# First cross attention: latent keys behind the context keys, latent values as one product over 96 stacked rows

## The reference, cut to what matters

```python
def _L0_xattn_ref(latents, context, Wq, Wk, Wv, Wo, q_norm_w, k_norm_w):
    HEADS, KV_HEADS, HEAD_DIM, EPS = 32, 8, 128, 1e-6
    kv = jnp.concatenate([context, latents], axis=1)      # 512 + 32 keys
    q = (latents @ Wq).reshape(...); k = (kv @ Wk).reshape(...); v = (kv @ Wv).reshape(...)
    q = rms_norm(q, q_norm_w); k = rms_norm(k, k_norm_w)
    scores = einsum('bhgqd,bhkd->bhgqk', qg, k) / sqrt(HEAD_DIM)
    probs = softmax(scores)                               # over all 544 keys
    out = einsum('bhgqk,bhkd->bhgqd', probs, v)
    return out @ Wo
```

## Time and profile before

| | us |
|---|---|
| Median of 3 runs (lowest, highest) | 1724.15 (1723.53, 1724.68) |
| Span of the profiled execution | 1722.3 |
| PE busy | 1599.7 (93%) |
| DVE busy | 900.3 (52%) |
| ACT busy | 610.9 (35%) |
| POOL busy | 349.7 (20%) |

### The profile page before, as it was taken

The page is one execution under the profiler, slowest core; times in us unless marked ns, Lnnn a source line. Parts: engine busy times, 40 slices in busy tenths (PEclk is TensorE's granted clock), DMA queues, the critical chain, the costliest instruction groups (busy, mean ns, idle before and its releaser), DMA issues. The chain is left out here.

```text
span 1722.3 us, 23860 instructions
## 1 busy us (share of the span) xinstructions
PE 1599.7 (93%) x8374; PEld 1325.3 (77%) x8374; DVE 900.3 (52%) x1704; ACT 610.9 (35%) x1036; POOL 349.7 (20%) x476
## 2 busy tenths in 40 slices
PE   6899999999999999978988899999999999876798
PEld 5678888888888887777546688888888888655686
DVE  5724454454544444565337355555555555556565
ACT  5523233332333333443126333333333333331343
POOL 3622111221112211041005421121121121101000
PEclk9999999999999999989579999999999999988899
DMA  7200000000000011252134000000000001230342
GB/s 258 74 28 27 9 20 20 8 27 8 20 20 8 27 51 50 98 202 91 58 114 154 7 26 13 12 24 12 12 24 14 11 25 50 97 118 0 133 162 86
DMA packets 25349, 94.57 MB, mean 55 GB/s; under 512 B 4422, under 2 KB 4550, under 8 KB 20680
## 3 DMA queue, kind: packets, MB, share of 16 engines
q1 hardware_dynamic: 25292, 93.82, 15.1%
HBM read 92.24 MB, written 1.57 MB: 54 GB/s over the span
## 5 line engine op out<-in xcount | busy, mean ns | idle before, releaser
L51 PE MATMUL c1a_kbanks<-c_wkv_lo_r,c_cT_hi 128*128 128x512 f32 x256 | 106.4, 416 | 3.5 <-PEq L368 3.5
L51 PE MATMUL c0a_kbanks<-c_wkv_lo_r,c_cT_hi 128*128 128x512 f32 x256 | 105.5, 412 | 1.5 <-PEq L368 1.5
L51 PE MATMUL c0a_vbank<-c_wkv_lo_r,c_cT_hi 128*128 128x512 f32 x256 | 105.1, 410 | 0.0
L968 DVE TENSOR_REDUCE c0a_ss<-c0a_sq 128x4 f32<-128x512 f32 x64 | 43.9, 685 | 116.4 <-ACT c0a_sq L888 102.3
L879 ACT ACTIVATE c0a_p<-c0a_sbank,c0a_nmax 128x544 f32<-128x544 f32 x62 | 44.5, 718 | 162.9 <-DVE c0a_nmax L922 162.9
L734 POOL TENSOR_TENSOR c0a_ms<-c0a_ss,c0a_const 128x4 f32<-128x4 f32 x64 | 12.7, 199 | 440.9 <-DVE c0a_ss L968 440.9
L968 DVE TENSOR_REDUCE c1a_ss<-c1a_sq 128x4 f32<-128x512 f32 x64 | 43.8, 685 | 111.5 <-ACT c1a_sq L888 111.5
L53 PE MATMUL c1a_kbanks<-c_wkv_hi,c_cT_lo_r 128*128 128x512 f32 x256 | 100.9, 394 | 0.0
L53 PE MATMUL c0a_kbanks<-c_wkv_hi,c_cT_lo_r 128*128 128x512 f32 x256 | 100.5, 393 | 0.0
L52 PE MATMUL c1a_kbanks<-c_wkv_hi,c_cT_hi 128*128 128x512 f32 x256 | 100.5, 392 | 0.0
L53 PE MATMUL c0a_vbank<-c_wkv_hi,c_cT_lo_r 128*128 128x512 f32 x256 | 100.1, 391 | 0.0
(11 more groups left out here) (461 smaller groups left out, 4442.2 us busy)
## 6 DMA issues: line engine op xcount, KB each, us to landing
g_stage<-in_l_wq SPq DMA_DIRECT2D x16, 1024.0 KB, 4.8
c_cT_lo<-in_ctx SPq DMA_DIRECT2D x64, 256.0 KB, 2.5
c_wkv_lo<-in_l_wo SPq DMA_DIRECT2D x16, 1024.0 KB, 4.8
e_stage<-in_e_w SPq DMA_DIRECT2D x20, 768.0 KB, 4.2
c_wkv_lo<-in_l_wkv SPq DMA_DIRECT2D x16, 512.0 KB, 5.5
m_stage<-in_mix_ffn SPq DMA_DIRECT2D x10, 768.0 KB, 4.3
m_traw<-in_mix_out SPq DMA_DIRECT2D x1, 1792.0 KB, 11.3
f_graw<-in_lora_g SPq DMA_DIRECT2D x1, 1536.0 KB, 7.3
```

What stands on the lines that cost most here:

```text
L51: nc.tensor.matmul(out, a[0], b[1], start=start, stop=False)
L968: nc.vector.tensor_reduce(ss[:, k % 2, :], sq[:, :].rearrange("p (h d) -> p h d", h=UNIT_H), AX.X, ALU.add).then_inc(k_summed, 1)
```

## The change: what it does

1. Latent keys. `kT` hi and lo get 544 columns for each head; POOL rounds the 32 latent keys of each head into the last 32 columns and subtracts for the rest (`latent_keys`, once for each unit, behind `q_lo`). `q_whole` and its copy go. `score` issues each of its three split products in two pieces of 272 columns, one in each bank of `sbank`. Maximum and exponential read two sides of 272.
2. Latent values. A rounded part and a rest are stored (two transfers of 1 MB; the rest is computed by DVE at the end of `queries`, `vl_rest`). `vlat` has 96 rows: hi, lo, hi, loaded by three transfers for each unit. The transposed latent probabilities stand beside it in `pTs`: hi, hi, rest. ACT writes the two rounded copies (`tail_heads`, between its copy of the values and that of the keys), DVE subtracts for the rest in place of its copy of 32 rows. `pv` ends with one fp32r matmul over 96 rows.
3. POOL and DVE wait for both stores at the start of `attend`, and in `finish` ACT's order is two exponentials, two `tail_heads`, then the output weights.

```diff
@@ queries
+                    sp.wait_ge(vl_rest, 2 * TT)
+                    for part in range(2):
+                        sp.dma_start(g["vlat_dram"][part].rearrange("(t p) n -> p t n", p=P),
+                                     as_f32(vl[:, part, :, :])).then_inc(vl_stored, 16)
...
+                if vl is not None:
+                    for j in range(2 * TT):
+                        half, t = divmod(j, TT)
+                        dve.wait_ge(vl_ready, j + 1)
+                        nc.vector.tensor_tensor(vl[:, 1, t, half * UW:(half + 1) * UW], pbank[j][:],
+                                                as_f32(vl[:, 0, t, half * UW:(half + 1) * UW]),
+                                                ALU.subtract).then_inc(vl_rest, 1)
@@ attend, SP
-                            sp.wait_ge(vl_stored, 16)
-                        sp.dma_start(vlat[:, hf, :],
+                            sp.wait_ge(vl_stored, 32)
+                        for row, part in enumerate((0, 1, 0)):
+                            sp.dma_start(as_f32(vlat[row * ROWS:(row + 1) * ROWS, hf, :]),
@@ attend, POOL
-                    if tail:
-                        nc.gpsimd.tensor_copy(flat(q_whole), mine)
...
+                def latent_keys(b, hf, u):
+                    own = klatT[:, hf * UNIT_H:(hf + 1) * UNIT_H, bass.ds(b * SEQ, SEQ)]
+                    nc.gpsimd.tensor_copy(kT[0][:, hf, :, CTX:KEYS], own).then_inc(kl_hi, 1)
+                    pool.wait_ge(const_set, 2)
+                    pool.wait_ge(kl_hi, u + 1)
+                    nc.gpsimd.tensor_tensor(kT[1][:, hf, :, CTX:KEYS], own, as_f32(kT[0][:, hf, :, CTX:KEYS]),
+                                            ALU.subtract).then_inc(kl_lo, 1)
...
+                if tail:
+                    pool.wait_ge(vl_stored, 32)
@@ attend, PE
-                    last = mm3(nc, bank[:, 0:CTX], tuple(h[:, ahf, k, :] for h in q),
-                               tuple(h[:, ahf, k, :] for h in kT), True, True)
                     if tail:
-                        last = nc.tensor.matmul(bank[:, CTX:KEYS], q_whole[:, ahf, k, :],
-                                                klatT[:, ahf * UNIT_H + k, bass.ds(at, SEQ)],
-                                                start=True, stop=True)
+                        for qp, kp in ((0, 1), (0, 0), (1, 0)):
+                            for side in range(2):
+                                last = nc.tensor.matmul(bank[:, side * CTX:side * CTX + HALF], q[qp][:, ahf, k, :],
+                                                        kT[kp][:, ahf, k, side * HALF:(side + 1) * HALF],
+                                                        start=(kp == 1), stop=(qp == 1))
...
-                        last = nc.tensor.matmul(bank[:, 0:HD], pT[0:SEQ, k % 2, CT, :],
+                        last = nc.tensor.matmul(bank[:, 0:HD], pTs[:, k % 2, :],
                                                 vlat[:, ahf, k * HD:(k + 1) * HD], start=False, stop=True)
@@ attend, ACT
+                def tail_heads(a, k, bank):
+                    act.wait_ge(pt_done, a + 1)
+                    need(act, o_done, a - 1)
+                    for row in range(2):
+                        nc.scalar.activation(pTs[row * ROWS:(row + 1) * ROWS, k % 2, :],
+                                             bank[0:SEQ, TAIL_T:TAIL_T + P], ACT.Copy).then_inc(pt_tail, 1)
@@ attend, DVE
                     if tail:
-                        last = nc.vector.tensor_copy(pT[0:SEQ, k % 2, CT, :], tail_bank[0:SEQ, TAIL_T:TAIL_T + P])
+                        dve.wait_ge(pt_tail, 2 * a + 2)
+                        last = nc.vector.tensor_tensor(pTs[2 * ROWS:STACK, k % 2, :],
+                                                       tail_bank[0:SEQ, TAIL_T:TAIL_T + P],
+                                                       as_f32(pTs[0:ROWS, k % 2, :]), ALU.subtract)
```

More of the change, by code:

```diff
@@ L620, in attend @@
         p = s.sb("p", [P, 2, KEYS])
-        pT = s.sb("pT", [P, 2, CT + 1, P])
+        pT = s.sb("pT", [P, 2, CT, P])
+        pTs = s.sb("pT_stack", [STACK, 2, P], F32R) if tail else None
         on = s.sb("on", [P, 2, HD])
@@ L673, in run, with sides @@
             finish()
+        def sides(bank):
+            return bank[:, :].rearrange("p (a n) -> p a n", a=2)[:, :, 0:HALF]
         def parts(b, hf):
@@ L826, in step @@
                             need(pe, pt_ready, a)
-                            score(a, sbank, ahf, k, (b - 1 if hf == 0 else b) * SEQ)
+                            score(a, sbank, ahf, k)
                         elif k > 0:
@@ L848, in finish @@
                     for k in range(2):
-                        score(LAST + k, scores[k], 1, k, at)
+                        score(LAST + k, scores[k], 1, k)
                     o_transpose(LAST - 1, 1, obank)
@@ L859, in finish @@
                             if k + 2 < UNIT_H:
-                                score(LAST + k + 2, scores[k % 2], 1, k + 2, at)
+                                score(LAST + k + 2, scores[k % 2], 1, k + 2)
                         for k in (pair, pair + 1):
@@ L877, in exponential @@
                     need(act, pt_done, a - 1)
-                    src = sm[:, k % 2, :] if mask is not None else bank[:, 0:KEYS]
-                    nc.scalar.activation(p[:, k % 2, :], src, ACT.Exp, bias=nmax[:, k:k + 1],
-                                         accum_out=rsum[:, k:k + 1]).then_inc(p_ready, 1)
+                    if mask is not None:
+                        src, dst = sm[:, k % 2, :], p[:, k % 2, :]
+                    else:
+                        src, dst = sides(bank), p[:, k % 2, :].rearrange("p (a n) -> p a n", a=2)
+                    nc.scalar.activation(dst, src, ACT.Exp, bias=nmax[:, k:k + 1],
+                                         accum_out=rsum[:, k:k + 1]).then_inc(p_ready, 1)
+                def tail_heads(a, k, bank):
+                    if not tail:
+                        return
+                    act.wait_ge(pt_done, a + 1)
[3 more added lines that the diff above has]
+                                             bank[0:SEQ, TAIL_T:TAIL_T + P], ACT.Copy).then_inc(pt_tail, 1)
                 def step(b, hf):
@@ L901, in finish @@
                 def finish():
-                    for k in range(UNIT_H):
-                        exponential(LAST + k, k, scores[k % 2])
-                        if k % 2:
-                            wo.make_hi(act, k // 2)
+                    for pair in range(0, UNIT_H, 2):
+                        for k in (pair, pair + 1):
+                            exponential(LAST + k, k, scores[k % 2])
+                        for k in (pair, pair + 1):
+                            tail_heads(LAST + k, k, scores[k % 2])
+                        wo.make_hi(act, pair // 2)
                 run(act, step, finish)
```

50 lines of the change are left out of this document (32 added, 18 removed).

## The result

The changed kernel takes 1686.95 us (median of 4 runs, 1686.35 to 1689.8), the kernel before, in runs on the same chip, 1724.41 (4 runs, 1723.53 to 1725.72). The ratio is 0.9781, 95% interval 0.9767 to 0.9795: faster by 2.2%. 1686 was forecast, with a range of 1678 to 1706. The profiled execution has a span of 1684.8 us, 37.5 less than before; forecast was 37.9.

The account below looks back on a forecast made before the run. PE, busy 537.76 of 540.00 us in `c0`'s steps, was taken as the bound. From the 1722.3 us span: -39.2 steps, -1 `finish`, +2.3 border = 1684.4; the median lies 1.85 above, so 1686, range 1678 to 1706.

Parts of the forecast that it names:

- The score: Score in `c0`'s steps: six 272-column fp32r pieces take 0.76 us instead of 1.03 with aftermath, saving 0.27 a step.
- The value tail: End of `pv`: one 96-row fp32r product costs 0.20 us instead of 0.59, saving 0.39 a step.
- the first fp32r behind fp32: Surcharge on the first fp32r matmul after fp32 ones: 0.09 us seen behind the old score, 0.08 put on the tail.
- the old product's 0.59: Old 32-row product in `pv`: 0.59 us, of which 0.17 lost ahead and 0.42 from its start to the score.
- R1: Value tail: 96 rows make PE drain as for 32; 17 us less gained, 1703 us; chance 0.12.
- R2: Ring ACT copies, keys, L912, `ot_place`, `pv` closes; PE waits some 0.3 us a step, 1704 us; chance 0.06.
- R3: Score: each of six pieces waits for its own weight load, 0.316 us a piece, 1755 us; chance 0.03.
- The border: Between the two blocks: two stores delay PE and DVE, a loss of 2.3 us, bounds 0.7 and 5.
- PE's later start: At the border: SP's wait for a DVE subtraction and a second store issue start PE 1.1 us later.
- the wait of 1.2 us ahead of the first `kt`: After the border: `kn` ends at 114.6, PE reaches the first `kt` at 113.4 and waits 1.2 us.
- or the clock falls in the longer idle stretch: At the border: one of the reasons given, with slower stores, for the upper bound of 5 us loss.
- `finish`: Remaining 5 `pv` and 4 scores, where PE waits for others: a gain of 1 us, 0 to 3.

Follow-up runs that it names:

- keys only: Changed kernel with the latent keys and six-piece score alone, old value tail kept: 1715.44 us, ratio 0.9951 to the kernel before.
- 512 + 32: Changed kernel with each split product of the score cut into pieces of 512 and 32 columns instead of two of 272: 1706.6 us, one run.
- 4 x 136: Changed kernel with the score in twelve pieces of 136 columns instead of six of 272: 1722.1 us, one run.
- 32 and 64 rows: Changed kernel with its last value product over only the first 32 or 64 of the 96 stacked rows: 1705.7 and 1714.8 us, one run each.
- eight more copies: Changed kernel with eight extra ACT copies of 32 x 64 behind the two, making ten, for which DVE waits: 1688.9 us, one run.
- the early stores: Changed kernel with the latent values stored in four halves, each issued as soon as its two banks are ready: 1688.46 us, ratio 0.9775.
- both removed: Changed kernel with the four early stores plus eight unused 128x512 products on PE behind the last query matmul: 1686.15 us, ratio 0.9756.
- the two halves: Changed kernel with only the keys part, 1715.44 us (ratio 0.9951), and with only the values part, 1696.28 us (ratio 0.9844).

## Why the prediction was right

**The bound.** PE is busy for 489.97 of 491.60 us at clock 1.00 in the steps, and it waits for nobody in them. So what the two parts save on PE arrives in full: 0.653 us a step against 0.66.

**The score**: 0.76 and no surcharge behind it was the step, 0.81 and none (0.24 against 0.227) is measured. A piece inside the row costs 0.125 as worked out from 256 and 512 columns (0.126). The first pair costs 0.31 instead of 0.25. Saved: 0.13 + 0.08 = 0.21, not 0.27. Of these 0.21 only 0.16 are the score's own (the step with keys only); 0.05 come with the 96 rows, for the 32-row product had slowed the score's first pair too.

**The value tail**: 0.14, not 0.20, and none of the gap: saved 0.45, not 0.39 (0.49 with what it takes off the score). Both misses are nearly one: I put 0.08 for "the first fp32r behind fp32" on the tail, and 0.06 falls on the next matmul. Nor is it the change of type. With 512 + 32 and with 4 x 136 all matmuls at that place are fp32r, and the value matmul behind still pays 0.08 and 0.06. What these places have in common is a short matmul ahead (32, 128 or 136 columns). That the longer one's weights then come late is the reading that fits; no experiment took the load apart from the matmul. The split of the old product's 0.59 was also off: "about 0.2" the product and "nearly 0.4" the change of rows. The runs give 0.29 for the rows (and 0.05 behind, in the score), 0.16 for plain fp32 and 0.14 for the product.

**R1** (96 rows turn the array) is refuted by 0.81 + 0.14. Its price was close: 0.29 a step was worked out, and 32 and 64 rows lengthen the step by 0.31 and 0.34. That is partly luck, since both terms of the difference (0.49 and 0.20) were 0.06 too high (0.43 and 0.14 measured). **R2** (the ring closes) is refuted: in the steps no load of `pv` waits for `ot_place`. The prediction counted the cover to the product; to the load, which is what waits, 0.78 us is left, and it took eight more copies to use that up. **R3** (loads not hidden) is refuted: pieces are 0.125 apart, with load records of 0.19, and pieces of 136 columns 0.112.

**The border**: +2.3 was forecast and +2.9 came, but by another way. PE's later start was right (+1.1; idle time grew by 1.29). The step that failed is the wait of 1.2 us ahead of the first `kt`. DVE is even 1.0 later than forecast (`kn` ends at 115.60, forecast 114.6), yet PE waits only 0.14, since it is itself 1.6 us late through the clock. I had that among the bounds ("or the clock falls in the longer idle stretch") and not in the sum. The clock's 1.6 and the wait for `kn` lie side by side, so removing the wait alone left the clock's part: with the early stores DVE is free, and the tile is still slow. Removing the clock's part alone was not run; with both removed the first `kt` comes 8.27 after PE's start, as before the change.

**`finish`**: 1 was taken, with a bound of 3, and it gave 3.4. Four scores and five tails at the steps' prices are 4 x 0.21 + 5 x 0.45 = 3.1 if all lay on the path. By the estimate from the two halves the change gave 2.4, inside the bound, and 1.0 is the clock that had fallen in the profile of before. Of the whole, then, about 1 us is no merit of the change.

The errors, +0.8 in the steps, +0.6 at the border, +0.4 in the queries, -2.4 in `finish` and +1.0 behind (untouched blocks, where the same kernel differed by 3.4), leave 0.4. 0.9 of the last lies in `c0`'s output block, which was granted a mean clock of 0.96 before and 0.92 after. That the sum is closer than its parts is luck: the gain in `finish` happens to pay for the others. The mechanism in the steps, which bring the whole net gain, was right. (The prediction's own range of 1679 to 1694 is a little narrower than its named bounds add up to, about 1677 to 1696.)

## What to carry to other kernels

Where one engine is busy for all of a loop, look for the instruction whose neighbours start late, and not for the one that lasts long: a product over few rows cost over 0.3 us beside its own time, and stacking the three terms of its split into one product of 96 rows took that away, for two small copies on an engine that had time to spare. Cut an uneven length into equal pieces as long as each stays above the time of the next one's weight load, and price a short piece with the start of the matmul behind it. When you count how much time a chain has before PE waits, count to the weight load and not to the product. At a border that leaves PE idle, read the granted clock of the first work behind it before you name a wait.

## What the runs showed of the hardware

- A product of 32 or of 64 rows between products of 128 rows costs 0.17 us ahead, 0.12 behind it and 0.03 to 0.05 more on the pair behind that; the step is 0.31 and 0.34 longer. One of 96 rows costs none of it.
- fp32r matmuls that each load new weights start 0.125 apart with 272 columns and 0.112 with 136. Behind a piece of 32 columns the next starts after 0.03, but its own 512 columns then take 0.32 and not 0.23.
- The weight load of `pv` waits for `ot_place`, not the product: with ten copies it stood idle 29 times, up to 0.17 late, and the step did not get longer.
- ACT copies of 32 x 64 from PSUM start 0.106 apart, with records of 0.20 to 0.22. The two of 32 x 128 take 0.29 each (0.58 until the next instruction), with records of 0.27. Why only the smaller ones overlap stays open.
- PE's clock behind a pause. At the border nine runs had 2.2 to 2.8 us without work, and in all nine the first tile ran partly at the 1.2 GHz level (the square 4.4 to 4.63 after PE's start); three had 0.4 to 1.5 and none did (3.02 to 3.04). In `finish` it is not so plain: before fell to it behind 1.50 us and the kernel with 32 rows behind 1.65 (granted clock 0.70 in the 5.6 us behind it); keys only did not behind 1.50, the change as it stands did not behind 1.64, and the kernel with ten copies did not behind 2.49. The length of the pause alone doesn't decide, and what else does stays open.
